# Output filter's channel half mixed on GpSimd and scaled earlier, and the map's six column mixes built on one shared difference

## The chip, the cores and the metric

The kernel runs on one core of one Trainium2 chip. The metric is the device time of one execution in microseconds (us). Before the change three runs took 116.66, 116.89 and 117.22 us; the median is 116.89 us.

## The reference, cut to what matters

Four layers follow each other on a map of 4 images, 128 channels and 16x16 pixels, all in float32. The change lies in the first, which has a spatial attention branch `xs` and a channel attention branch `xc`, and ends with a 3x3 convolution of both:

```python
xs = bn_relu(conv2d(x, w_sam, 1), ...)      # 3x3 convolution
xs = sam(xs, w_qk, w_v, gamma_sam)          # softmax over 256 pixels, per image
xc = bn_relu(conv2d(x, w_cam, 1), ...)      # 3x3 convolution
xc = cam(xc, gamma_cam)                     # softmax over 128 channels, per image
xcat = jnp.concatenate([xs, xc], axis=1)
return conv2d(xcat, w_out, 1)               # 3x3, 256 -> 128 channels
```

`w_out` has two halves: `out_s` works on the spatial branch and `out_c` on the channel branch. The later layers (masked bottleneck, latent attention, a full attention over 256 pixels) are untouched.

## The kernel before, in words

All channels lie on the 128 partitions, so every map of one image is 128x256. The 3x3 convolutions are computed in a transformed form along the width, with three matmuls (one per filter row) for each transformed column set. The output convolution uses sets of four columns: six mixes of the six map columns around each group of four, six mixes of the three filter columns, and an inverse on the results. So before `out_conv` can run, three things have to be made:

- the six mixes of each half of each map, `mixed["s"]` and `mixed["c"]`, by VectorE (DVE) in `mix_columns_six` (L590 to L617). It is called as `s_mixed(0)`, `s_mixed(1)`, `c_mixed(0)`, `c_mixed(1)`, each for two images. Every call has 12 instructions: six read the wide map with a step of four columns (L602 to L605, L612, L613) and write contiguous scratch tiles, and six combine these (L607 to L611, L615, L617).
- four mixes of the filter columns, `w_mix[n]` 0 to 3. Mixes 0 and 1 need the raw columns alone (`mix_weights`). Mixes 2 and 3 need two raw columns scaled by ScalarE (ACT) in `scale_weights` (L427 to L431), and then three more sums (`mix_weights_two`). For `cam` and `out_s` GpSimd (POOL) does this (L329 to L346); for `out_c` DVE does (L619 to L639, called at L765 and L770).
- the other two filter mixes are the raw columns.

Nothing is scheduled by a tool. Each engine has its own program, written out by hand, and runs it in that order; waits are on counters (`wait_ge`). What matters around the change:

- PE (TensorE) interleaves the convolution of `cam` with the spatial attention, and then the output convolution of the spatial half with the channel attention. `s_transpose(b)` (L1132) turns the probabilities of image b once DVE has normalised them; `s_apply(b)` (L1139) waits for ACT's copy of the turned ones; `c_gram(i)` (L1161), `c_transpose(i)` (L1170) and `c_apply(i)` (L1178) are the channel attention of half i.
- DVE runs `s_norm(b)` (L688: one reciprocal, two scalings of 128x256), then `join_outer` of `cam` half 0 (L653), `s_mixed(0)`, `s_residual(2)` and `(3)` (L696), `s_mixed(1)`, `c_max(0)` (L708), `join_inner` of `cam` half 1, `c_norm(0)`, and so on through L739 to L772.
- ACT runs `s_exp(3)`, `s_turned(2)`, `relu_in("cam", 0, ...)` (which waits for L653), `s_turned(3)`, then the channel attention's steps, in which `scale_weights("out_c")` stands after `c_turned(0)` (L459).
- POOL mixes the weights of `cam` and `out_s`, writes one part of `keys` (L348) and is then free until L352, at 79.22 us of the span.

Of the kernel before, what the change touches and what calls it, by code (L numbers as in the profile page):

```python
# [79 lines left out]
def build(nc, x, w_sam, w_cam, w_out, early, late, out):  # L80
    with ExitStack() as ctx:
# [238 lines left out]
        def _(pool):  # L320
# [18 lines left out]
            n, done = "out_s", ev["out_s_w"]  # L339
            pool.wait_ge(ev["out_s_scaled"], 2)  # L340
            pool.wait_ge(done, 3)
            nc.gpsimd.tensor_tensor(w_sum[n][:, :], w_mix[n][:, 2, :], w_mix[n][:, 3, :], ALU.add).then_inc(done, 1)
            pool.wait_ge(done, 4)
            nc.gpsimd.tensor_tensor(w_mix[n][:, 2, :], w_sum[n][:, :], w_raw[n][:, 1, :], ALU.add).then_inc(done, 1)
            nc.gpsimd.tensor_tensor(w_mix[n][:, 3, :], w_sum[n][:, :], w_raw[n][:, 1, :],
                                    ALU.subtract).then_inc(done, 1)  # L346
# [225 lines left out]
        def _(dve):  # L572
# [17 lines left out]
            def mix_columns_six(n, i):  # L590

                d = wide_map[n][:, 2 * i:2 * i + 2, :, :].rearrange("p b h w -> p (b h) w")
                at = [d[:, :, k:k + 4 * (WQ - 1) + 1:4] for k in range(6)]
# [10 lines left out]
                nc.vector.tensor_tensor(four(c), at[4], at[2], ALU.subtract).then_inc(diff, 1)  # L604
                nc.vector.tensor_tensor(four(e), at[3], at[1], ALU.subtract).then_inc(diff, 1)  # L605
                dve.wait_ge(diff, 6 * i + 2)
# [2 lines left out]
                dve.wait_ge(diff, 6 * i + 4)
# [4 lines left out]
                dve.wait_ge(diff, 6 * i + 5)  # L614
                nc.vector.scalar_tensor_tensor(to(0), images(f), 4.0, images(c), ALU.mult, ALU.add).then_inc(done, 1)  # L615
                dve.wait_ge(diff, 6 * i + 6)
                nc.vector.scalar_tensor_tensor(to(5), images(e), 4.0, images(h), ALU.mult, ALU.add).then_inc(done, 1)  # L617

            def mix_weights(n):  # L619
# [8 lines left out]
                                        ALU.subtract).then_inc(done, 1)  # L628

            def mix_weights_two(n):  # L630

                done = ev[f"{n}_w"]
                dve.wait_ge(ev[f"{n}_scaled"], 2)
                dve.wait_ge(done, 3)
                nc.vector.tensor_tensor(w_sum[n][:, :], w_mix[n][:, 2, :], w_mix[n][:, 3, :], ALU.add).then_inc(done, 1)
                dve.wait_ge(done, 4)
# [924 lines left out]
```

## Time and profile before

| | |
|---|---|
| median of three runs | 116.89 us |
| the profiled execution | 117.24 us |
| its span, first to last instruction | 115.4 us |
| PE busy | 107.2 us, 93% |
| DVE busy | 79.1 us, 68% |
| ACT busy | 50.6 us, 44% |
| POOL busy | 16.8 us, 15% |

The span is what the rows below count from. The profiled execution took 1.84 us more than its span, and 0.35 us more than the median. A group of instructions is read as busy time, number and mean duration; a line of the timeline as start, duration, engine, line of the kernel, and in brackets how long the engine sat idle before and what released it. Instructions of one engine overlap slightly, so the distance between starts is less than a duration.

### The profile page before, as it was taken

What the parts mean: (1) busy time and instruction counts of PE and PEld (TensorE: products, weight loads), DVE (VectorE), ACT (ScalarE), POOL (GpSimd) and SP (SyncE); (2) the same over time, 40 slices, a digit from 0 to 9 for tenths busy, and PEclk for the clock granted to TensorE, in tenths of its full rate; (3) what the DMA queues carried; (4) which work ended last, traced back from release to release, by engine and by line L of the source; (5) the groups of instructions that cost most, each with busy time, mean ns of one, the idle gap of its engine ahead of it and who ended that gap; (6) DMA issues with size and microseconds to landing.
All of it is one profiled execution on the core that took longest, in us unless ns stands there. A gap on an engine that the chain in (4) does not pass through costs nothing.

```text
span 115.4 us, 2010 instructions
## 1 busy us (share of the span) xinstructions
PE 107.2 (93%) x699; PEld 91.3 (79%) x699; DVE 79.1 (68%) x249; ACT 50.6 (44%) x147; POOL 16.8 (15%) x28
## 2 busy tenths in 40 slices
PE   5999998989999999989997889998999999999980
PEld 5988887858868989989986579696799997776570
DVE  1756568479899897876967332659564796779960
ACT  5150495997242344130121401014785618769730
POOL 5007995000000000000000000004300002233000
PEclk9999999999999999999999999999999999999999
DMA  3999900000000000000000000000000000000122
GB/s 90 291 354 410 408 31 6 0 0 0 3 0 0 0 3 6 0 0 0 6 0 0 0 0 0 9 0 0 0 0 0 0 6 0 0 0 0 45 70 72
DMA packets 3321, 5.22 MB, mean 45 GB/s; under 512 B 496, under 2 KB 2928, under 8 KB 3184
## 3 DMA queue, kind: packets, MB, share of 16 engines
q1 hardware_dynamic: 3168, 5.09, 12.6%
q8 instruction: 6, 0.10, 0.4%
q10 hardware_dynamic: 144, 0.01, 0.1%
q14 instruction: 3, 0.02, 0.1%
HBM read 4.57 MB, written 0.52 MB: 44 GB/s over the span
## 4 chain that ended last, share of the span: by engine, by line
PE 76%; DVE 11%; ACT 8%; issue 2%; DVEq 0%; ACTq 0%
PE psum L1019 15%; PE psum L1037 9%; PE psum L1103 7%; PE psum L1288 4%; PE psum L1356 4%; PE psum L1330 4%; PE psum L1348 3%; PE psum L1144 2%; PE psum L1401 2%; PE psum L1414 2%; PE psum L1323 2%; PE psum L1242 2%; PE psum L1434 2%; PE psum L1181 2%; PE psum L1338 2%
## 5 line engine op out<-in xcount | busy, mean ns | idle before, releaser
L352 POOL TENSOR_TENSOR att_s<-xc,x 128x256 f32<-128x256 f32 x3 | 2.2, 727 | 61.0 <-DVE xc L891 61.0
L1103 PE MATMUL psum<-spin 128*128 128x256 f32 x50 | 8.9, 336 | 1.2 <-DVE spin L577 1.2
L1103 PEld LDWEIGHTS psum<-spin 128*128 128x128 f32 x50 | 7.8, 233 | 1.5 <-DVE spin L577 1.2
L1019 PE MATMUL psum<-mixed_x,w_raw_sam 128*128 128x256 f32 x24 | 6.8, 436 | 0.0
L358 POOL TENSOR_SCALAR att_c<-x,gbv 128x256 f32<-128x256 f32 x4 | 3.8, 961 | 19.3 <-DVE x L940 19.3
L1019 PE MATMUL psum<-mixed_x,w_mix_cam 128*128 128x256 f32 x24 | 6.4, 384 | 0.0
L1037 PE MATMUL psum<-mixed_s,w_mix_out_s 128*128 128x128 f32 x48 | 6.2, 275 | 0.0
L1019 PE MATMUL psum<-mixed_x,w_raw_cam 128*128 128x256 f32 x24 | 6.2, 379 | 0.0
L1019 PEld LDWEIGHTS psum<-mixed_x,w_raw_sam 128*128 128x128 f32 x24 | 5.4, 231 | 0.9
L1037 PEld LDWEIGHTS psum<-mixed_s,w_mix_out_s 128*128 128x128 f32 x48 | 5.9, 192 | 0.1
L1037 PE MATMUL psum<-mixed_c,w_mix_out_c 128*128 128x128 f32 x48 | 5.7, 275 | 0.0
L1037 PEld LDWEIGHTS psum<-mixed_c,w_mix_out_c 128*128 128x128 f32 x48 | 5.5, 192 | 0.0
L1019 PE MATMUL psum<-mixed_x,w_mix_sam 128*128 128x256 f32 x24 | 5.3, 379 | 0.0
L1356 PE MATMUL psum<-prob,par 128*128 128x128 f32 x32 | 5.2, 286 | 0.1
L587 DVE TENSOR_TENSOR mixed_x<-wide_x 128x256 f32<-128x256 f32 x8 | 3.7, 521 | 2.3 <-DMA wide_x<-in_x 2.3
L914 DVE SCALAR_TENSOR_TENSOR prob<-psum,rinv,par 128x128 f32<-128x128 f32 x16 | 4.9, 347 | 0.3
L1019 PEld LDWEIGHTS psum<-mixed_x,w_mix_sam 128*128 128x128 f32 x24 | 4.6, 190 | 0.6
L1330 PE MATMUL psum<-keys,xc 128*128 128x272 f32 x16 | 4.6, 408 | 0.5 <-ACT keys L492 0.5
L902 DVE TENSOR_REDUCE nmax<-psum 128x2 f32<-128x512 f32 x4 | 2.8, 692 | 3.0 <-PE psum L1330 3.0
L1288 PE MATMUL psum<-hpad,par 128*128 128x256 f32 x18 | 4.2, 384 | 0.6 <-DVE hpad L830 0.6
L1019 PEld LDWEIGHTS psum<-mixed_x,w_raw_cam 128*128 128x128 f32 x24 | 4.3, 190 | 0.5
L1356 PEld LDWEIGHTS psum<-prob,par 128*128 128x128 f32 x32 | 4.2, 191 | 0.3 <-DVE prob L914 0.3
(245 smaller groups left out, 268.8 us busy)
## 6 DMA issues: line engine op xcount, KB each, us to landing
par<-in_late SPq DMA_DIRECT2D x1, 1406.0 KB, 8.0
wide_x<-in_x SPq DMA_DIRECT2D x2, 288.0 KB, 3.9
w_raw_sam<-in_w_sam SPq DMA_DIRECT2D x3, 192.0 KB, 3.5
w_raw_cam<-in_w_cam SPq DMA_DIRECT2D x3, 192.0 KB, 5.1
w_raw_out_s<-in_w_out SPq DMA_DIRECT2D x3, 192.0 KB, 5.2
w_raw_out_c<-in_w_out SPq DMA_DIRECT2D x3, 192.0 KB, 5.1
out<-y SPq DMA_DIRECT2D x2, 128.0 KB, 2.0
out<-y SPq DMA_DIRECT2D x4, 64.0 KB, 2.3
```

Source lines behind the costliest of these rows:

```text
L358: nc.gpsimd.tensor_scalar(x3b[:, b, :], x3[:, b, :], gbv[:, 0:1], None, ALU.add).then_inc(ev["f_xb"], 1)
L587: nc.vector.tensor_tensor(mixed[n][:, k, 2 * i:2 * i + 2, 1:1 + H, :], at[a], at[b], op).then_inc(done, 1)
L902: nc.vector.tensor_reduce(nmax[:, b, :], psum[:, 2 * b:2 * b + 2, L:L + HW], AX.X, ALU.max, negate=True).then_inc(ev["n_max"], 1)
L914: nc.vector.scalar_tensor_tensor(wide[:, b, i, 0:P].rearrange("p (m l) -> p m l", m=M8), o[:, L1 * i:L1 * i + L].unsqueeze(1).broadcast_to ...
L1019: return mm(o[:, c:c + HW].rearrange("p (b s) -> p b s", b=2), w[:, C * dy:C * (dy + 1)], mixed[src][:, i, 2 * half:2 * half + 2, dy:dy + ...
L1037: return mm(o[:, c:c + HALF].rearrange("p (b s) -> p b s", b=2), w[:, C * dy:C * (dy + 1)], mixed[src][:, i, 2 * half:2 * half + 2, dy:dy ...
L1103: mm(bank[k][:, 0:HW], spin[:, 0:P], spin[:, :], start=True, stop=True, skip_group_check=True)
L1144: m = mm(bank[4 + b % 2][:, 0:HW], vt[:, b, j, :], pt_sb[:, b, j, :], start=(j == 0), stop=(j == NCH - 1))
L1288: m = mm(o, par1[:, a + P * t:a + P * (t + 1)], hpad[:, dy:dy + H, dx:dx + W], start=(t == 0), stop=(t == NT - 1))
L1330: m = mm(bank[2 * b + i][:, 0:L + HW], pixels(x2, b, i), keys[:, b, :], start=True, stop=True)
L1348: m = mm(bank[2 * b][:, L1 * i:L1 * (i + 1)], pt_sb[:, b, j, P * i:P * (i + 1)], gt[:, b, j, :], start=(j == 0), stop=(j == NCH - 1))
L1356: m = mm(o[:, 0:HW].rearrange("p (m i c) -> p i m c", i=NCH, c=L)[:, i, :, :], p1("w_o_rep"), wide[:, b, i, 0:P].rearrange("p (m c) -> p m ...
```

## The change

Three edits:

1. GpSimd mixes the weights of `out_c` too. `mix_weights` and `mix_weights_two` become functions on POOL and are called for `out_c` right after `out_s`, before the copy to `keys`. Both are gone from DVE for `out_c` (six instructions of 128x384).
2. ACT's `scale_weights("out_c")` moves from after `c_turned(0)` to after `s_exp(3)`, before `s_turned(2)`.
3. `mix_columns_six` subtracts the map from itself two columns on, once over all 16 columns of every row (128x512), into `mix_t`; the mixes 3, 4, 0 and 5 take every fourth column of that. This replaces four differences of 128x128. The sixth mix comes out with the opposite sign, which the inverse takes back (-1.0 becomes 1.0 in `join_six`).

```diff
@@ gpsimd @@
+            mix_weights("cam")
+            mix_weights("out_s")
+            mix_weights_two("out_s")
+            mix_weights("out_c")
+            mix_weights_two("out_c")
             pool.wait_ge(d_late, 16)
@@ scalar @@
             s_exp(3)
+            scale_weights("out_c")
             s_turned(2)
...
             c_turned(0)
-            scale_weights("out_c")
@@ vector, mix_columns_six @@
+                t = mix_t[n]
+                tk = [t[:, k:2 * H * W:4].rearrange("p (b s) -> p b s", b=2) for k in range(4)]
...
-                nc.vector.tensor_tensor(four(c), at[4], at[2], ALU.subtract).then_inc(diff, 1)
-                nc.vector.tensor_tensor(four(e), at[3], at[1], ALU.subtract).then_inc(diff, 1)
+                nc.vector.tensor_tensor(t[:, :].rearrange("p (r w) -> p r w", w=W), d[:, :, 2:2 + W], d[:, :, 0:W],
+                                        ALU.subtract).then_inc(diff, 1)
...
-                nc.vector.scalar_tensor_tensor(to(3), images(e), 2.0, images(c), ALU.mult, ALU.add).then_inc(done, 1)
-                nc.vector.scalar_tensor_tensor(to(4), images(e), -2.0, images(c), ALU.mult, ALU.add).then_inc(done, 1)
-                nc.vector.tensor_tensor(four(f), at[0], at[2], ALU.subtract).then_inc(diff, 1)
-                nc.vector.tensor_tensor(four(h), at[3], at[5], ALU.subtract).then_inc(diff, 1)
...
-                nc.vector.scalar_tensor_tensor(to(0), images(f), 4.0, images(c), ALU.mult, ALU.add).then_inc(done, 1)
...
-                nc.vector.scalar_tensor_tensor(to(5), images(e), 4.0, images(h), ALU.mult, ALU.add).then_inc(done, 1)
+                nc.vector.scalar_tensor_tensor(to(3), tk[1], 2.0, tk[2], ALU.mult, ALU.add).then_inc(done, 1)
+                nc.vector.scalar_tensor_tensor(to(4), tk[1], -2.0, tk[2], ALU.mult, ALU.add).then_inc(done, 1)
+                nc.vector.scalar_tensor_tensor(to(0), tk[0], -4.0, tk[2], ALU.mult, ALU.add).then_inc(done, 1)
+                nc.vector.scalar_tensor_tensor(to(5), tk[1], -4.0, tk[3], ALU.mult, ALU.add).then_inc(done, 1)
@@ vector, the steps @@
-            mix_weights("out_c")
             c_residual(0)
...
-            mix_weights_two("out_c")
             c_residual(1)
```

The order on POOL, from the last sums of `out_s` on. Before (`w_sum`, `w_mix` and `w_raw` are the sums, the mixed and the raw filter columns; the names behind "waits" are the counters):

```order
L337 TENSOR_TENSOR w_mix_out_s<-w_sum_out_s,w_raw_out_s 128x384
L342 TENSOR_TENSOR w_sum_out_s<-w_mix_out_s 128x384 [waits out_s_w,out_s_scaled]
L344 TENSOR_TENSOR w_mix_out_s<-w_sum_out_s,w_raw_out_s 128x384 [waits out_s_w]
L345 TENSOR_TENSOR w_mix_out_s<-w_sum_out_s,w_raw_out_s 128x384
L348 COPY keys<-par 128x4x16 [waits d_late]
```

and now (the line numbers are those of the changed kernel):

```order
L349 TENSOR_TENSOR w_mix_out_s<-w_sum_out_s,w_raw_out_s 128x384
L334 TENSOR_TENSOR w_sum_out_c<-w_raw_out_c 128x384 [waits d_w_out_c2,d_w_out_c0]
L337 TENSOR_TENSOR w_mix_out_c<-w_sum_out_c,w_raw_out_c 128x384 [waits out_c_w,d_w_out_c1]
L338 TENSOR_TENSOR w_mix_out_c<-w_sum_out_c,w_raw_out_c 128x384
L346 TENSOR_TENSOR w_sum_out_c<-w_mix_out_c 128x384 [waits out_c_w,out_c_scaled]
L348 TENSOR_TENSOR w_mix_out_c<-w_sum_out_c,w_raw_out_c 128x384 [waits out_c_w]
L349 TENSOR_TENSOR w_mix_out_c<-w_sum_out_c,w_raw_out_c 128x384
L358 COPY keys<-par 128x4x16 [waits d_late]
```

Six sums of 128x384 have come between the sums of `out_s` and the copy to `keys`; the fourth of them waits for ACT's scaling.

The order on ACT, from the exponentials of the last image of the spatial attention on. Before:

```order
L401 ACTIVATE prob,rsum<-psum,nmax 128x256 [waits s_max]
L401 ACTIVATE prob,rsum<-psum,nmax 128x256
L407 COPY pt_sb<-psum 128x512 [waits s_tp]
L384 ACTIVATE xc<-eo,bn_shift,bn_inv 128x2x256 [waits cam_y,bn_step]
L407 COPY pt_sb<-psum 128x512 [waits s_tp]
L411 COPY att_c<-psum 128x512 [waits c_yt]
L378 COPY m_sb<-psum 128x256 [waits cam_inner]
```

and now:

```order
L411 ACTIVATE prob,rsum<-psum,nmax 128x256 [waits s_max]
L411 ACTIVATE prob,rsum<-psum,nmax 128x256
L441 ACTIVATE w_mix_out_c<-w_raw_out_c 128x384 [waits d_w_out_c0]
L441 ACTIVATE w_mix_out_c<-w_raw_out_c 128x384 [waits d_w_out_c2]
L417 COPY pt_sb<-psum 128x512 [waits s_tp]
L394 ACTIVATE xc<-eo,bn_shift,bn_inv 128x2x256 [waits cam_y,bn_step]
L417 COPY pt_sb<-psum 128x512 [waits s_tp]
L421 COPY att_c<-psum 128x512 [waits c_yt]
```

The two scalings now stand ahead of the copy of image 2's turned probabilities, and with it ahead of the ReLU of `cam` half 0.

The order on DVE in the first `mix_columns_six`. Before:

```order
L602 SCALAR_TENSOR_TENSOR mix_ab_s<-wide_s 128x128 [waits s_att]
L603 SCALAR_TENSOR_TENSOR mix_ab_s<-wide_s 128x128
L604 TENSOR_TENSOR mix_fech_s<-wide_s 128x128
L605 TENSOR_TENSOR mix_fech_s<-wide_s 128x128
L607 TENSOR_TENSOR mixed_s<-mix_ab_s 128x2x64 [waits s_diff]
L608 TENSOR_TENSOR mixed_s<-mix_ab_s 128x2x64
L610 SCALAR_TENSOR_TENSOR mixed_s<-mix_fech_s 128x2x64 [waits s_diff]
L611 SCALAR_TENSOR_TENSOR mixed_s<-mix_fech_s 128x2x64
L612 TENSOR_TENSOR mix_fech_s<-wide_s 128x128
L613 TENSOR_TENSOR mix_fech_s<-wide_s 128x128
L615 SCALAR_TENSOR_TENSOR mixed_s<-mix_fech_s 128x2x64 [waits s_diff]
L617 SCALAR_TENSOR_TENSOR mixed_s<-mix_fech_s 128x2x64 [waits s_diff]
```

and now:

```order
L614 SCALAR_TENSOR_TENSOR mix_ab_s<-wide_s 128x128 [waits s_att]
L615 SCALAR_TENSOR_TENSOR mix_ab_s<-wide_s 128x128
L616 TENSOR_TENSOR mix_t_s<-wide_s 128x512
L619 TENSOR_TENSOR mixed_s<-mix_ab_s 128x2x64 [waits s_diff]
L620 TENSOR_TENSOR mixed_s<-mix_ab_s 128x2x64
L622 SCALAR_TENSOR_TENSOR mixed_s<-mix_t_s 128x2x64 [waits s_diff]
L623 SCALAR_TENSOR_TENSOR mixed_s<-mix_t_s 128x2x64
L624 SCALAR_TENSOR_TENSOR mixed_s<-mix_t_s 128x2x64
L625 SCALAR_TENSOR_TENSOR mixed_s<-mix_t_s 128x2x64
```

Three instructions fewer; the last four now read `mix_t` with a step of four.

## Rows read from the trace of the kernel before

**Rows 1.** Chain that ended last, in order of time: start us, us, what.

```profile
48.21 0.34 DVE cmax L711
```

**Rows 2.** Timeline, 40 to 75 us: DVE, ACT and PE in the channel attention.

```profile
42.96 0.93 ACT L431 ACTIVATE w_mix_out_c<-w_raw_out_c 128x384 f32<-128x384 f32 x2
...
44.29 0.75 DVE L728 SCALAR_TENSOR_TENSOR wide_c<-psum,par,xc 128x512 f32<-128x512 f32 x1 [0.82 <-PE psum L1181]
...
46.75 1.06 PE L1166 MATMUL psum<-att_c 128*128 128x128 f32 x8
...
48.12 0.43 DVE L711 TENSOR_REDUCE cmax<-psum 128x2 f32<-128x256 f32 x1
...
50.23 0.55 DVE L635 TENSOR_TENSOR w_sum_out_c<-w_mix_out_c 128x384 f32<-128x384 f32 x1
...
50.36 0.44 PE L1175 MATMUL psum<-par,cprob 128*128 128x128 f32 x2 [0.32 <-DVE cprob L723]
...
53.05 0.75 DVE L728 SCALAR_TENSOR_TENSOR wide_c<-psum,par,xc 128x512 f32<-128x512 f32 x1 [1.21 <-PE psum L1181]
```

**Rows 3.** Groups of DVE by line and shape, 36 to 75 us.

```profile
L723 DVE TENSOR_SCALAR cprob<-cprob,cinv 128x128 f32<-128x128 f32 x4 | 1.0, 282 | 0.1
...
L602 DVE SCALAR_TENSOR_TENSOR mix_ab_c<-wide_c 128x128 f32<-128x128 f32 x2 | 0.8, 396 | 0.1
...
L610 DVE SCALAR_TENSOR_TENSOR mixed_c<-mix_fech_c 128x128 f32<-128x128 f32 x2 | 0.6, 290 | 0.0
...
L627 DVE TENSOR_TENSOR w_mix_out_c<-w_sum_out_c,w_raw_out_c 128x384 f32<-128x384 f32 x1 | 0.6, 553 | 0.0
```

**Rows 4.** Timeline, 22 to 41 us: ACT, DVE and PE in the spatial attention.

```profile
22.45 0.41 DVE L677 SCALAR_TENSOR_TENSOR qst<-psum,qst 32x256 fp32r<-32x256 f32 x1 [0.86 <-ACT qst L390]
...
28.67 0.22 ACT L401 ACTIVATION_READ_ACCUMULATOR prob<-psum,nmax 128x1 f32 x1
...
30.01 0.62 DVE L693 TENSOR_SCALAR prob<-prob,rinv 128x256 f32<-128x256 f32 x2
...
30.45 0.59 ACT L407 COPY pt_sb<-psum 128x512 f32<-128x512 f32 x1 [1.55 <-PE psum L1096]
...
30.68 0.60 PE L1096 MATMUL psum<-par,prob 128*128 128x128 f32 x4
30.88 0.75 DVE L653 SCALAR_TENSOR_TENSOR eo<-pq,psum 128x256 f32<-128x256 f32 x2 [0.26 <-PE psum L1019]
...
31.55 0.39 DVE L602 SCALAR_TENSOR_TENSOR mix_ab_s<-wide_s 128x128 f32<-128x128 f32 x1
...
33.09 1.13 PE L1144 MATMUL psum<-pt_sb,vt 128*128 128x256 f32 x4
...
34.60 0.86 DVE L699 SCALAR_TENSOR_TENSOR wide_s<-psum,par,xs 128x256 f32<-128x256 f32 x2
...
39.02 0.42 DVE L711 TENSOR_REDUCE cmax<-psum 128x2 f32<-128x256 f32 x1 [0.39 <-PE psum L1166]
```

**Rows 5.** Timeline, 3 to 22 us: the last sum of out_s on POOL.

```profile
17.73 0.99 POOL L345 TENSOR_TENSOR w_mix_out_s<-w_sum_out_s,w_raw_out_s 128x384 f32<-128x384 f32 x1
```

**Rows 6.** Timeline of DVE, 76 to 83 us: L891 without and with POOL at work.

```profile
78.72 0.42 DVE L891 SCALAR_TENSOR_TENSOR xc<-gate,xs 128x256 f32<-128x256 f32 x1
...
79.51 0.72 DVE L891 SCALAR_TENSOR_TENSOR xc<-gate,xs 128x256 f32<-128x256 f32 x1
```

**Rows 7.** Timeline of POOL, 78 to 83 us.

```profile
79.22 0.73 POOL L352 TENSOR_TENSOR att_s<-xc,x 128x256 f32<-128x256 f32 x1 [60.32 <-DVE xc L891]
```

**Rows 8.** Source L587, the column mixes of x on DVE: duration ns min/median/max.

```profile
L587 DVE TENSOR_TENSOR mixed_x<-wide_x x8: 418/420/1225, 3.7 to 9.4; 128x256 f32<-128x256 f32 x8
```

**Rows 9.** Source L693, the scalings of the spatial attention: ns min/median/max.

```profile
L693 DVE TENSOR_SCALAR prob<-prob,rinv x8: 346/351/354, 21.0 to 30.3; 128x256 f32<-128x256 f32 x8
```

**Rows 10.** Source L965, the same operation in the last layer: ns min/median/max.

```profile
L965 DVE TENSOR_SCALAR prob<-prob,rinv x4: 346/354/485, 101.0 to 106.2; 128x256 f32<-128x256 f32 x4
```

**Rows 11.** Timeline of POOL, 75 us to the end.

```profile
100.99 1.07 POOL L358 TENSOR_SCALAR att_c<-x,gbv 128x256 f32<-128x256 f32 x1 [2.03 <-DVE x L940]
```

More of the change, by code:

```diff
@@ L116, in build @@
         mixed.update({n: sb(f"mixed_{n}", [P, 6, B, HP, WQ]) for n in ("s", "c")})
-        mix_fech = {n: sb(f"mix_fech_{n}", [P, 4, HALF]) for n in ("s", "c")}
+        mix_t = {n: sb(f"mix_t_{n}", [P, 2 * H * W]) for n in ("s", "c")}
         mix_ab = {n: sb(f"mix_ab_{n}", [P, 2, HALF]) for n in ("s", "c")}
@@ L327, in _, with mix_weights @@
             nc.gpsimd.memset(hpad[:, :, :], 0.0).then_inc(ev["zeroed"], 1)
-            for n in ("cam", "out_s"):
+            def mix_weights(n):
                 done = ev[f"{n}_w"]
@@ L338, in _, with mix_weights_two @@
                                         ALU.subtract).then_inc(done, 1)
[L339 to L346, printed above, removed]
+            def mix_weights_two(n):
+                done = ev[f"{n}_w"]
+                pool.wait_ge(ev[f"{n}_scaled"], 2)
+                pool.wait_ge(done, 3)
+                nc.gpsimd.tensor_tensor(w_sum[n][:, :], w_mix[n][:, 2, :], w_mix[n][:, 3, :], ALU.add).then_inc(done, 1)
+                pool.wait_ge(done, 4)
+                nc.gpsimd.tensor_tensor(w_mix[n][:, 2, :], w_sum[n][:, :], w_raw[n][:, 1, :], ALU.add).then_inc(done, 1)
+                nc.gpsimd.tensor_tensor(w_mix[n][:, 3, :], w_sum[n][:, :], w_raw[n][:, 1, :],
+                                        ALU.subtract).then_inc(done, 1)
+            mix_weights("cam")
[3 more added lines that the diff above has]
+            mix_weights_two("out_c")
             pool.wait_ge(d_late, 16)
@@ L593, in mix_columns_six @@
                 at = [d[:, :, k:k + 4 * (WQ - 1) + 1:4] for k in range(6)]
-                f, e, c, h = [mix_fech[n][:, k, :] for k in range(4)]
                 a, b = [mix_ab[n][:, k, :] for k in range(2)]
@@ L603, in mix_columns_six @@
                 nc.vector.scalar_tensor_tensor(four(b), at[1], -4.0, at[3], ALU.mult, ALU.add).then_inc(diff, 1)
[L604 to L606 removed]
+                nc.vector.tensor_tensor(t[:, :].rearrange("p (r w) -> p r w", w=W), d[:, :, 2:2 + W], d[:, :, 0:W],
+                                        ALU.subtract).then_inc(diff, 1)
+                dve.wait_ge(diff, 3 * i + 2)
                 nc.vector.tensor_tensor(to(1), images(a), images(b), ALU.add).then_inc(done, 1)
                 nc.vector.tensor_tensor(to(2), images(a), images(b), ALU.subtract).then_inc(done, 1)
[L609 to L617 removed]
+                dve.wait_ge(diff, 3 * i + 3)
+                nc.vector.scalar_tensor_tensor(to(3), tk[1], 2.0, tk[2], ALU.mult, ALU.add).then_inc(done, 1)
+                nc.vector.scalar_tensor_tensor(to(4), tk[1], -2.0, tk[2], ALU.mult, ALU.add).then_inc(done, 1)
+                nc.vector.scalar_tensor_tensor(to(0), tk[0], -4.0, tk[2], ALU.mult, ALU.add).then_inc(done, 1)
+                nc.vector.scalar_tensor_tensor(to(5), tk[1], -4.0, tk[3], ALU.mult, ALU.add).then_inc(done, 1)
             def mix_weights(n):
@@ L627, in mix_weights @@
                 nc.vector.tensor_tensor(w_mix[n][:, 1, :], w_sum[n][:, :], w_raw[n][:, 1, :],
[L628 to L636, printed above, removed]
-                nc.vector.tensor_tensor(w_mix[n][:, 2, :], w_sum[n][:, :], w_raw[n][:, 1, :], ALU.add).then_inc(done, 1)
-                nc.vector.tensor_tensor(w_mix[n][:, 3, :], w_sum[n][:, :], w_raw[n][:, 1, :],
                                         ALU.subtract).then_inc(done, 1)
@@ L811, in join_six @@
                 dve.wait_ge(ev["out_last"], 2 * i + 2)
-                nc.vector.scalar_tensor_tensor(phase(x1, i, 3), o[:, HALF:HW], -1.0, last[:, i, 1, :], ALU.mult,
+                nc.vector.scalar_tensor_tensor(phase(x1, i, 3), o[:, HALF:HW], 1.0, last[:, i, 1, :], ALU.mult,
                                                ALU.add).then_inc(ev["x1_done"], 1)
```

## Prediction

> **What bounds the kernel now.** I read the chain of waits first: it follows PE nearly everywhere and leaves it only where PE sits waiting. So an edit on another engine is worth what it takes from a wait of PE. I then went through the timeline from 22 to 63 us, where all three edits act, and looked only at PE's idle brackets. Two belong to the change. Before `s_apply(3)`, at 33.09 us, PE waited 0.48 us for ACT's copy of the turned probabilities; that copy stands behind the ReLU, the ReLU behind DVE's L653 at 30.88 us [rows 4]. Before `c_transpose(1)`, at 50.36 us, PE waited 0.32 us for DVE's `c_norm(1)` [rows 2]. The second wait begins in `c_mixed(0)`: the chain passes through `c_max(1)` at 48.2 us [rows 1], and DVE came to it straight from the mixing, without an idle bracket, though `c_gram(1)` had ended at 46.75 + 1.06 = 47.81 us [rows 2].
>
> **The change, part by part.** The sum is made against the profiled execution (117.24 us, span 115.4), which lies 0.35 us above the median of 116.89; I carry the difference over to the median.
>
> *Weights of `out_c` off DVE:* six sums of 0.55 us [rows 3]. Worth nothing: after the first three DVE idled 0.82 us until PE released `c_residual(0)` at 44.29 us, and after the other three (from 50.23 us) it idled 1.21 us until 53.05 us [rows 2]. That cover remains, with more room in it.
>
> *Mixing:* a call takes 34.60 - 31.55 = 3.05 us for 12 instructions [rows 4]. An instruction that reads with a step of four lasts 396 ns, one that reads contiguous scratch 290 ns [rows 3]; from start to start this is about 0.31 and 0.20 us (estimates: each less the overlap of 0.09), and 6 x 0.31 + 6 x 0.20 = 3.06 agrees. Now there are two of the first kind, two of the second, four combinations that read `mix_t` with a step of four, and one subtraction of 128x512. A sum of 128x384 takes 553 ns [rows 3]; 128 elements more at 130 ns (below), less the overlap, give 0.60. The four combinations lie between 0.20 (contiguous) and 0.31 (stepped); I take 0.31, because what rows 3 tell apart is the step of the reads. 2 x 0.31 + 2 x 0.20 + 4 x 0.31 + 0.60 = 2.86 us, 0.19 saved a call; with 0.20 it is 2.42, 0.63 saved. `c_mixed(0)` takes the 0.19 off PE's wait at 50.36 us; more than 48.12 - 47.81 = 0.31 us can't be had there, since `c_gram(1)` is then the later one. `c_mixed(1)` ends long before PE needs it. So this edit is worth **-0.19 us** (bounds -0.31 and 0). The Trainium skill's page "SBUF — State Buffer" (note on cache lines, section "Door 1: The DMA port swizzle") gives "4 fp32" as how far one can step for free. Read so, the combinations would cost 0.20 and the term would be -0.31; the 396 against 290 ns of rows 3 speak against it.
>
> *Scaling on ACT:* two instructions, 0.93 us together [rows 2], in the gap from 28.89 us to the copy at 30.45 us, of which 1.55 us are idle [rows 4]. They end near 29.82 us. Worth nothing where they go and nothing where they leave.
>
> *Weights on POOL:* a sum takes 0.99 us there; the last of `out_s` ends at 18.72 us [rows 5], and the first three of `out_c` follow until 21.8 us. The next three can't start before ACT's scaling has ended. A POOL instruction that waits starts 0.08 us after its releaser (79.22 us against 78.72 + 0.42 [rows 6, 7]): so from 29.9 us, the fifth sum 0.08 us after the fourth, the sixth right behind, undisturbed until 33.0 us, then the copy to `keys` (first read near 80 us). The weights are due at 53.3 us. The duration is covered by 20 us; what counts is what DVE does meanwhile. From 30.01 us it runs the two scalings of `s_norm(3)`, L653, and from 31.55 us `s_mixed(0)` [rows 4].
>
> The trace shows what happens when a POOL sum of two SBUF tensors runs beside a DVE instruction with two SBUF inputs. L891 took 0.42 us alone and 0.72 us when started at 79.51 us beside a POOL sum that ran from 79.22 to 79.95 us [rows 6, 7]: it ended 0.28 us after POOL did, so it did its reading after POOL's end. L587, two SBUF inputs as well, lasted 1225 ns once against 420 [rows 8], beside a POOL sum of the weights. So the instructions of `s_mixed(0)` will be held. For `s_norm(3)` there is no such row: its instruction has one SBUF tensor as input. But it takes 351 ns for 256 elements and 283 for 128 [rows 9, 3], 68 ns per 128, where two-input instructions take 420 - 290 = 130: it moves two elements at a time, so it uses the second path too. Below, its cost is bounded by L965, the same operation, which beside a POOL instruction with one input took 485 ns at most instead of 354, with POOL's at 1072 ns [rows 10, 11]: 0.13 us. Above, by L891: held until POOL's sum has ended. I take the upper one, since POOL's operation is then the same, and it is POOL's that decides how long. The Trainium skill has it as a rule (page "SBUF — State Buffer", section "Who interferes with whom"): an exclusive lock, held for a whole instruction, that a scalar operation of VectorE in its two-port mode takes as well; rows 6 to 8 agree, rows 10 and 11 only in part.
>
> With that: POOL's fourth sum holds from 29.9 to 30.9 us. The first scaling of `s_norm(3)`, due at 30.01, moves its elements until 30.9 + 2 x 0.07 = 31.04 and ends near 31.1. POOL's fifth sum has been ready since 30.98, and goes first; the second scaling ends near 32.3 instead of 30.63 us. L653 then runs from 32.25 to 33.0 (one input in PSUM, not held), the ReLU of 0.86 us from 33.05 to 33.9, ACT's copy to 34.4, and PE starts `s_apply(3)` at 34.4 instead of 33.09: **+1.3 us**. PE's waits from there on have their causes behind this point and shift with it. Is `s_mixed` late too? From 33.05 us, held until 33.3 and once more by the copy to `keys` (0.25), it ends near 36.4; two residuals of 0.9 in all and `s_mixed(1)` of 2.86 lead to 40.2 us, while `c_gram(0)`, which ended near 38.99, has moved to 40.3. Just hidden.
>
> Sum: 1.3 - 0.19 = +1.1 us: 118.3 us for the profiled execution, **118.0 us** for the median.
>
> The first three sums meet only `s_norm(0)` at 20.97 us, which may end 0.7 us late, at 22.3; DVE idled 0.86 us until L677 at 22.45 us [rows 4], and PE turns these probabilities after 23 us. Nothing.
>
> **The rivals.**
>
> *A. POOL keeps the path through its fifth and sixth sum,* which follow each other without a gap. The second scaling then ends near 33.3 us: +2.3 - 0.19, 119.0 us. Against it: L587, of which one instruction was held and not two. 0.08.
>
> *B. DVE gets both scalings in a row after the fourth sum.* `s_norm(3)` ends near 31.4 us, L653 0.55 us late; then `s_mixed(0)` meets the last two sums, ends near 36.2, and `c_max(0)` comes at 39.8 instead of 39.02 us [rows 4]. +0.75 - 0.19, 117.5 us. For it: the two are queued one behind the other, and the decision falls within 0.1 us. 0.13.
>
> *C. `s_norm(3)` is not held* (the 0.13 us of rows 10), only `s_mixed(0)`. Due at 31.55 us, it waits until 32.0, again from 32.3 to 33.3, and 0.2 for the copy: it ends near 36.1 with its own 0.19 saved, against 34.60 us. `c_max(0)` had 0.39 us to spare, and `s_mixed(1)` gives 0.19: 1.3 to 1.5 - 0.39 - 0.19, some +0.8, less 0.19 later, +0.6 at most; if the holds are shorter, +0.4: 117.3 us. 0.23.
>
> *D. Not slower: the collisions fall into DVE's slack.* Between 31.55 us and `c_max(0)` DVE has 0.39 us idle and 2 x 0.19 saved, 0.77 us. If POOL and DVE take turns at some 0.13 us an instruction, as in rows 10 and 11, this covers them, and only the gain at 50.36 us remains: 116.7 us. This decides from the point where DVE loses less than 0.77 us in all, and nothing before L653. Against it: rows 6 to 8, three times the full hold. 0.12.
>
> That the change doesn't do what it says is excluded by the order of the instructions. Faster by more than 0.58 us would need two of PE's waits to fall that no edit touches.
>
> **How the numbers follow.** The forecast has 0.42; 0.02 is left for what no row suggests. Half a per cent, 0.58 us, is about what a measurement of this kernel can tell from no change: the bounds are 116.31 and 117.47 us. Slower: the forecast, A, half of B and a small part of C, 0.59. Same: the rest of B and C, nearly all of D, 0.35. Faster 0.06, the part of D where stepped reads are cheap, and the unknown. Range: 116.6 takes in D and 118.7 the forecast with 0.7 us on top; A is left out, with a little at either end.
>
> **What would show it.** In the profile after: the scalings of image 3 lasting over 1 us (the first to near 31.1, the second to near 32.3 us); PE waiting some 1.3 us or more on either side of `s_apply(3)` for ACT; a scaling of image 0 of about 1 us, harmless; the combinations from `mix_t` at 0.39 us; the wait before `c_transpose(1)` at 0.1 to 0.15 us. It would be wrong if the scalings of image 3 stay at 0.35 us (C or D), or if the sums on POOL, and not the DVE instructions, grow longer.

## The result, and the profile after

| | before | after |
|---|---|---|
| median of 20 runs each | 116.83 us | 117.52 us |
| ratio of the two, 95% interval | | 1.0052 [1.0031, 1.0074] |
| the same, measured again with the experiments | 116.72 us | 117.85 us, 1.0082 [1.0041, 1.0123] |
| a profiled execution, its span | 117.24 us, 115.4 us | 117.59 us, 115.7 us |
| DVE busy | 68% | 66% |
| POOL busy | 15% | 20% |

By the ratios the change makes the kernel slower by 0.6 us (0.5%), by 1.0 us in the second measurement. The forecast was +1.1 us. Some runs of nearly every kernel (8 of these 20 after) had a lower granted clock for a few us from 72 us or later and took 1.4 to 3.3 us more, so the ratios leave them out, the rows here are from a second profile of the changed kernel, whose granted clock was 0.999, and an experiment whose profile was such a run has no milestone for the keys below.

The timeline of the changed kernel, 28 to 52 us, on ACT, POOL, DVE, PE and PE's weight loads (PEld). Columns as ahead of the prediction; L690 are the scalings, L650 is `join_outer`, L394 the ReLU of `cam`, L417 the copy of the turned probabilities, L1139 `s_apply`, L1170 and L1176 `c_transpose` and `c_apply`.

```profile
28.29 0.95 ACT L441 ACTIVATE w_mix_out_c<-w_raw_out_c 128x384 f32<-128x384 f32 x2
29.32 1.00 POOL L346 TENSOR_TENSOR w_sum_out_c<-w_mix_out_c 128x384 f32<-128x384 f32 x1 [8.13 <-ACT w_mix_out_c L441]
29.54 0.94 DVE L690 TENSOR_SCALAR prob<-prob,rinv 128x256 f32<-128x256 f32 x1
30.39 1.15 DVE L690 TENSOR_SCALAR prob<-prob,rinv 128x256 f32<-128x256 f32 x1
30.40 0.99 POOL L348 TENSOR_TENSOR w_mix_out_c<-w_sum_out_c,w_raw_out_c 128x384 f32<-128x384 f32 x1
30.59 0.20 PEld L1091 LDWEIGHTS psum<-par,prob 128*128 128x128 f32 x2 [0.62 <-ACT pt_sb L417]
31.35 1.05 POOL L349 TENSOR_TENSOR w_mix_out_c<-w_sum_out_c,w_raw_out_c 128x384 f32<-128x384 f32 x1
31.47 0.74 DVE L650 SCALAR_TENSOR_TENSOR eo<-pq,psum 128x256 f32<-128x256 f32 x2
31.60 0.20 PEld L1091 LDWEIGHTS psum<-par,prob 128*128 128x128 f32 x2 [0.81 <-DVE prob L690]
32.13 0.53 DVE L614 SCALAR_TENSOR_TENSOR mix_ab_s<-wide_s 128x128 f32<-128x128 f32 x1
32.30 0.87 ACT L394 ACTIVATE xc<-eo,bn_shift,bn_inv 128x512 f32<-128x512 f32 x1 [1.74 <-DVE eo L650]
33.05 0.56 ACT L417 COPY pt_sb<-psum 128x512 f32<-128x512 f32 x1
33.66 0.73 PEld L1139 LDWEIGHTS psum<-pt_sb,vt 128*128 128x128 f32 x4 [0.30 <-ACT pt_sb L417]
...
39.59 0.42 DVE L708 TENSOR_REDUCE cmax<-psum 128x2 f32<-128x256 f32 x1 [0.64 <-PE psum L1161]
...
41.69 0.75 DVE L650 SCALAR_TENSOR_TENSOR eo<-pq,psum 128x256 f32<-128x256 f32 x2
...
42.86 0.85 ACT L394 ACTIVATE xc<-eo,bn_shift,bn_inv 128x512 f32<-128x512 f32 x1 [1.80 <-DVE eo L650]
44.00 1.13 PE L1176 MATMUL psum<-xc,cpt 128*128 128x256 f32 x4 [0.40 <-ACT cpt L432]
...
47.17 0.29 DVE L619 TENSOR_TENSOR mixed_c<-mix_ab_c 128x128 f32<-128x128 f32 x1
...
47.58 0.40 DVE L622 SCALAR_TENSOR_TENSOR mixed_c<-mix_t_c 128x128 f32<-128x128 f32 x1
...
48.53 2.40 PE L1032 MATMUL psum<-mixed_s,w_mix_out_s 128*128 128x128 f32 x20
...
51.03 0.20 PEld L1170 LDWEIGHTS psum<-par,cprob 128*128 128x128 f32 x2 [0.30 <-DVE cprob L720]
51.04 0.44 PE L1170 MATMUL psum<-par,cprob 128*128 128x128 f32 x2
```

**The hold** stands in the first ten rows. POOL's fourth sum runs from 29.32 to 30.32 us; the first scaling of image 3, begun at 29.54, ends at 30.48, 0.16 us after it. The fifth sum runs from 30.40 to 31.39; the second scaling ends at 31.54, 0.15 us after that. Before, the pair took 0.62 us [rows 4]; now the two take 2.00 us. PE's weight loads stand idle twice in `s_transpose(3)`, for 0.62 and 0.81 us, and its matmuls for 0.24 and 0.57 us (the first bracket names ACT's copy, but before that row the program also waits for the first scaling, and the kernel before began the same row while ACT's copy of image 2 was still running: 30.48 against 30.45 + 0.59 us), and `s_mixed(0)` is held once more, L614 taking 0.53 us beside the sixth sum. `c_max(0)` (L708) still waits for PE, 0.64 us against 0.39 [rows 4], so DVE's lateness is over by then. **The mixing**: reads of `mix_t` with a step of four take 0.40 us and contiguous ones 0.29 us.

**What the forecast didn't have** stands at 42.86 us: the ReLU of `cam` half 1 starts 0.42 us after L650 ended (41.69 + 0.75 = 42.44). The ReLU of half 0 starts 0.09 us after its own L650 (31.47 + 0.74 = 32.21, and 32.30). The first profile of the changed kernel has the same 0.42 us. The chain of waits calls it "issue", a wait for nothing that the profile shows:

```profile
41.77 0.67 DVE eo L650 x2
42.45 0.02 issue
42.47 0.02 ACTq L393
42.48 0.38 issue
42.86 0.85 ACT xc L394
```

**Where the time goes.** PE's milestones, counted in every trace from the start of `s_transpose(1)` (first column, in us of the span); the last column is the rest of the span behind the first matmul of the latent attention's keys (L1323 before, L1318 after).

| kernel | start | s_apply(3) | c_transpose(0) | c_apply(0) | c_transpose(1) | keys | rest |
|---|---|---|---|---|---|---|---|
| before | 24.37 | 8.72 | 16.89 | 18.75 | 25.99 | 54.49 | 36.5 |
| before, second profile | 24.19 | 8.72 | 16.88 | 18.74 | 25.99 | 54.47 | 36.3 |
| after | 23.91 | 9.76 | 17.92 | 20.09 | 27.13 | 55.62 | 36.2 |

Between start and keys the change costs 1.13 us, in three steps: **+1.04** before `s_apply(3)`, **+0.31** between `c_transpose(0)` and `c_apply(0)` (2.17 us instead of 1.86), and **-0.20** before `c_transpose(1)` (7.04 instead of 7.24). Two profiles of one kernel agree there to 0.02 us, while start and rest vary by 0.2 us and more between profiles of one kernel; so the experiments are read from this table.

### The profile page after: what moved, and what is told of

The parts are those of the page before. It is cut to its first block, busy times and chain, and to the rows that moved or that the text cites. A ratio compares the mean times of both kernels' runs of the same rounds, so it can differ in the third digit from the quotient of the medians.

```text
span 118.7 us, 1998 instructions
## 1 busy us (share of the span) xinstructions
PE 109.8 (93%) x699; PEld 93.5 (79%) x699; DVE 77.3 (65%) x231; ACT 50.3 (42%) x147; POOL 23.0 (19%) x34
## 4 chain that ended last, share of the span: by engine, by line
PE 73%; DVE 13%; ACT 7%; issue 3%; DVEq 0%; ACTq 0%
PE psum L1014 13%; PE psum L1098 9%; PE psum L1032 8%; PE psum L1325 4%; PE psum L1283 4%; PE psum L1351 3%; PE psum L1343 3%; PE psum L1396 2%; PE psum L1409 2%; PE psum L1429 2%; PE psum L1176 2%; PE psum L1139 2%; PE psum L1333 2%; PE psum L1361 2%; PE psum L1318 2%
## 5 line engine op out<-in xcount | busy, mean ns | idle before, releaser
L1098 PE MATMUL psum<-spin 128*128 128x256 f32 x50 | 11.2, 397 | 1.2 <-DVE spin L587 1.2
L1098 PEld LDWEIGHTS psum<-spin 128*128 128x128 f32 x50 | 9.9, 293 | 1.8 <-DVE spin L587 1.2
L725 DVE SCALAR_TENSOR_TENSOR wide_c<-psum,par,xc 128x512 f32<-128x512 f32 x2 | 1.5, 752 | 5.5 <-PE psum L1176 5.5
```

Of the source, the lines that this page charges most:

```text
L1098: mm(bank[k][:, 0:HW], spin[:, 0:P], spin[:, :], start=True, stop=True, skip_group_check=True)
```

## The experiments

### The changed kernel again, and the kernel before again

Both unchanged, for traces and times beside those of the experiments.

> The changed kernel once more, for its time and for a second trace. Hold theory (POOL's fourth and fifth sums hold the two scalings of image 3): +0.4 to +0.9 us against the kernel before, the two scalings again near 2.0 us together and s_apply(3) about 1.05 us late against the work ahead of it. Rival, ACT stalls: in the first trace ACT started the ReLU of cam half 1 0.42 us after its releaser where it was 0.10 before; if that is part of the change, it is there again and worth 0.3 us, if it was chance it is gone.

Measured: 117.85 us, 1.0082 [1.0041, 1.0123], so +0.5 to +1.4 us. Its rows are those above; the hold and the late ReLU are both there again.

> The kernel before once more, for a second trace: the first trace reached s_transpose(1) at 24.37 us of its span, four traces of other kernels at 22.96 to 24.07 us, though nothing of the change acts ahead of it. If this is chance of the loads, this trace lies among those, near 23.7 us, and from s_transpose(1) to the end it takes the same 91.0 us as the first. If the changed kernels really start earlier, it comes out near 24.4 again. Time: the same as before, within 0.3 us.

Measured: 116.68 us, 1.0012 [0.9978, 1.0045]; its milestones are the second row of the table.

### The mixing alone

`mix_columns_six` as in the change, everything else as before.

> Only the mixing of the map by one difference; the weights of out_c stay on DVE and ACT's scaling where it was. Hold theory: -0.2 us (0.19 a call, of which c_mixed(0) gives its own to PE). Rival, the mixing is what costs (stepped reads slower than the differences they replace): +0.3 us or more.

Measured: 116.39 us, 0.9964 [0.9929, 0.9999]. Milestones: start 22.96; 8.73, 16.89, 18.75, 25.78. The scalings of image 3 are back at 0.62 us and the ReLU of half 1 starts 0.09 us after its releaser. The whole effect in the trace is -0.21 us before `c_transpose(1)`, the forecast's -0.19; the ratio, 0 to -0.8 us, agrees but can't tell the size. The timeline of the kernel with the mixing alone, 45 to 49 us:

```profile
45.30 0.38 DVE L612 SCALAR_TENSOR_TENSOR mixed_c<-mix_t_c 128x128 f32<-128x128 f32 x1
45.60 0.38 DVE L613 SCALAR_TENSOR_TENSOR mixed_c<-mix_t_c 128x128 f32<-128x128 f32 x1
...
46.24 2.40 PE L1035 MATMUL psum<-mixed_s,w_mix_out_s 128*128 128x128 f32 x20
48.74 0.44 PE L1173 MATMUL psum<-par,cprob 128*128 128x128 f32 x2
```

From start to start a combination takes 0.30 us. PE's row of `c_transpose(1)` prints no idle bracket any more, but the row before it ends at 48.64 us (46.24 + 2.40), so 0.10 us of the 0.32 [rows 2] is left.

### The weights alone

The mixing as before; the weights of `out_c` on POOL and the scaling on ACT as in the change.

> Only the weights of out_c on POOL with ACT's scaling after s_exp(3); the map is mixed by the old twelve instructions. Hold theory: slower by 0.2 us more than the full change, so +0.6 to +1.1 us. Rival, the mixing is what costs: 0 to +0.2 us.

Measured: 118.19 us, 1.0139 [1.0088, 1.0190]: +1.6 us, more than the +0.6 to +1.1 expected. Milestones: start 23.63; 9.65, 17.81, 19.98, 27.24, keys 56.10. Both costs are here (the late ReLU too: 2.17 us between `c_transpose(0)` and `c_apply(0)`), without the mixing's gain. Two more stand in its timeline. In the attention of image 0 POOL's third sum starts 0.69 us after DVE's first scaling (20.80 and 20.11 us), where in the changed kernel it starts 0.32 us ahead of it (20.20 and 20.52 us). So two sums hold the two scalings (1.89 us for the pair, where the changed kernel takes 1.09):

```profile
19.84 1.00 POOL L337 TENSOR_TENSOR w_mix_out_c<-w_sum_out_c,w_raw_out_c 128x384 f32<-128x384 f32 x1
20.11 1.89 DVE L692 TENSOR_SCALAR prob<-prob,rinv 128x256 f32<-128x256 f32 x2
20.80 1.04 POOL L338 TENSOR_TENSOR w_mix_out_c<-w_sum_out_c,w_raw_out_c 128x384 f32<-128x384 f32 x1
...
77.20 0.23 DVE L873 SCALAR_TENSOR_TENSOR gate<-gate,cm3q 128x64 f32<-128x64 f32 x1 [1.09 <-ACT gate L491]
77.88 0.43 DVE L881 TENSOR_TENSOR xs<-psum,gate 128x256 f32<-128x256 f32 x1 [0.46 <-DVE gate L873]
...
79.73 0.70 PE L1320 MATMUL psum<-xc,w_keys 128*128 128x256 f32 x2 [0.34 <-ACT xc L497]
```

`s_transpose(1)` is 0.12 us late by that (PE's bracket is 0.30 us, 0.18 in the changed kernel), so the start from which the milestones count is itself late and they come out too small by as much: the forecast's "harmless" scaling of image 0 (1.09 us in the changed kernel) is so only while POOL's third sum starts early enough. The second is PE's wait of 0.34 us before the keys at 79.73 us, where neither edit works. It comes from DVE: L881 starts 0.45 us after its releaser, DVE's own L873, has ended (77.20 + 0.23 = 77.43, and 77.88), where the changed kernel has 0.08 us there. This looks like the late ReLU, on another engine whose program is shorter by the sums taken off it; no run tested that.

### The scaling on ACT later: nothing for POOL to do until then

```diff
             s_exp(3)
-            scale_weights("out_c")
...
             c_exp(0)
+            scale_weights("out_c")
             relu_in("cam", 1, 1, xc, ev["xc_done"])
```

> The full change, but ACT scales the weights of out_c after the exponentials of c_exp(0), so that POOL's last three sums run from about 41.5 to 44.6 us, where DVE reads PSUM or waits. Hold theory: the scalings of image 3 back at 0.35 us each, and the gain of the mixing left alone: -0.2 us against before, 0.8 us under the full change. Rival, it is POOL's first three sums, or the loss of DVE's own sums, or code that lies elsewhere: as slow as the full change, +0.5 us. Rival, ACT's scaling now delays the ReLU behind it: the wait before c_apply(0) grows by up to 0.9 us.

Measured: 116.66 us, 1.0007 [0.9967, 1.0046]. Milestones: start 23.59; 8.73, 16.90, 19.06, 26.08, keys 54.57. POOL's three sums run from 40.61 to 43.66 us, the scalings of image 3 take 0.62 us, and the +1.04 is gone: it was the hold. The expected gain of 0.2 us isn't in the trace, because the ReLU starts 0.41 us after L650's end again. It now stands right behind the scaling, but the scaling doesn't delay it: ACT had been idle for 0.96 us. That sent me to its place in ACT's program.

### Two small copies on ACT

The ReLU of half 1 has two more ACT instructions ahead of it in the changed kernel than before (the scaling's). Three kernels put two copies of 128x1 on ACT behind `s_exp(3)`, in a gap of 1.55 us [rows 4]: one with the mixing alone, one with the later scaling, one with the whole change.

```diff
             s_exp(3)
+            for k in range(2):
+                nc.scalar.copy(pad_out[:, k:k + 1], p0("gam_sam"))
```

> The mixing alone, and two copies of 128x1 on ACT after s_exp(3), in ACT's idle gap, which do nothing but shift ACT's later instructions by two places, as the moved scaling does. Theory P (the extra 0.31 us before c_apply(0) comes from the place of the ReLU of cam half 1 in ACT's program): the 0.31 us appear here too, and eat the gain of the mixing: +0.1 us against before instead of -0.2. Rival (it comes from POOL or from DVE being less busy): no such gap, -0.2 us as with the mixing alone.

> The version with the scaling after c_exp(0), with the same two copies of 128x1 on ACT, so that the ReLU stands four places later than before, not two. Theory P: the 0.31 us go from the ReLU to another instruction; if that one is not waited for, -0.2 us against before, otherwise as the version without them (0.0). Rival: no change.

> The full change with ACT's two copies of 128x1 after its scaling. Theory P: 0.3 us faster than the full change, the wait before c_apply(0) gone; what is left is the hold less the mixing, 1.04 - 0.21 = +0.8 us from s_transpose(1) to the end. Rival (the first two terms are not additive, the hold also feeds the later wait): as slow as the full change.

| kernel | ratio, 95% | ACT instructions more ahead of the ReLU | ReLU after L650's end | c_transpose(0) to c_apply(0) | keys |
|---|---|---|---|---|---|
| mixing alone | 0.9964 [0.9929, 0.9999] | 0 | 0.09 | 1.86 | |
| with two copies | 1.0041 [1.0006, 1.0077] | 2 | 0.42 | 2.17 | 54.57 |
| later scaling | 1.0007 [0.9967, 1.0046] | 2 | 0.41 | 2.16 | 54.57 |
| with two copies | 0.9978 [0.9932, 1.0024] | 4 | 0.10 | 1.85 | 54.26 |
| whole change | 1.0082 [1.0041, 1.0123] | 2 | 0.42 | 2.17 | 55.62 |
| with two copies | 1.0082 [1.0041, 1.0123] | 4 | 0.09 | 1.86 | 55.46 |

The timeline of ACT and DVE, 40 to 44 us; with the mixing alone and two copies:

```profile
40.84 0.74 DVE L654 SCALAR_TENSOR_TENSOR eo<-pq,psum 128x256 f32<-128x256 f32 x2
...
42.00 0.86 ACT L385 ACTIVATE xc<-eo,bn_shift,bn_inv 128x512 f32<-128x512 f32 x1 [1.79 <-DVE eo L654]
...
43.15 1.13 PE L1182 MATMUL psum<-xc,cpt 128*128 128x256 f32 x4 [0.39 <-ACT cpt L423]
```

and with the whole change and two copies:

```profile
41.52 0.75 DVE L653 SCALAR_TENSOR_TENSOR eo<-pq,psum 128x256 f32<-128x256 f32 x2
...
42.36 0.86 ACT L395 ACTIVATE xc<-eo,bn_shift,bn_inv 128x512 f32<-128x512 f32 x1 [1.47 <-DVE eo L653]
```

Two copies in an idle gap some 13 us earlier put the 0.31 us into a kernel without it, and take it out of two kernels with it. So it depends on the ReLU's place in ACT's program. The other kernels here agree: 0.41 us with two instructions more (the weights alone, POOL only writing), 0.10 us with four (the last three below). What lies beneath was not found. This reading rests on the traces: the ratios move by +0.9, -0.3 and 0.0 us from row to row of a pair, and with intervals of 0.4 to 0.5 us to either side they can't show 0.31 us.

The whole change with copies gained only 0.16 us at the keys, and nothing by its ratio, where 0.3 us were expected: the copies stand before the scaling and make POOL's fourth sum later against DVE (29.16 us, where the pair of scalings starts at 29.19 and takes 2.19 us), so `s_apply(3)` comes at 9.94 instead of 9.76. POOL is later against DVE by 0.19 us and `s_apply(3)` by 0.18: the hold answers to the time of POOL's sums, nearly one to one.

### POOL only writes

```diff
+                if n == "out_c":
+                    for k in range(3):
+                        nc.gpsimd.memset(fill[:, k, :], 0.0).then_inc(done, 1)
+                    return
```

> The full change with POOL's last three sums for out_c left out; in their place, behind the same waits, three fills of 128x1100 with zeros of about 1 us each, which read nothing. The mixes 2 and 3 of out_c are so never finished. Hold theory: what holds DVE is POOL's reading; then the instructions of s_mixed(0), with two inputs, are not held at all. For the scalings of image 3, which move two elements at a time, reads and writes may both count: held as before (2.0 us together) if POOL's writes are enough, 0.62 us together if not. Rival (DVE is slowed by whatever POOL does): both are held.

This kernel leaves out the last three sums of `out_c`, so its mixes 2 and 3 stay unfinished. One run, 120.74 us at a granted clock of 0.971; only its timeline, 28 to 36 us, is read:

```profile
29.84 3.28 POOL L349 MEMSET fill<- 128x1100 f32 x3 [8.46 <-ACT w_mix_out_c L446]
...
30.08 2.09 DVE L695 TENSOR_SCALAR prob<-prob,rinv 128x256 f32<-128x256 f32 x2
...
32.74 0.39 DVE L619 SCALAR_TENSOR_TENSOR mix_ab_s<-wide_s 128x128 f32<-128x128 f32 x1
```

The pair of scalings is held as long by POOL's writes (2.09 us) as by its sums, so it isn't reads alone that hold them. L619, with two inputs in SBUF, takes its usual 0.39 us while the third fill still runs. The Trainium skill's page "SBUF — State Buffer" (section "Who interferes with whom") has both: VectorE's two-port mode, in which a scaling moves two elements at a time, meets anything GpSimd does, two SBUF inputs meet only its reads. These rows agree.

### The scaling of image 3 in a form that isn't held

```diff
+                if b == 3:
+                    for i in range(NCH):
+                        nc.vector.tensor_scalar(prob[:, b, i, :], prob[:, b, i, :], rinv[:, b, i:i + 1], 0.0,
+                                                ALU.mult, ALU.add, accum_out=unused[:, i:i + 1]).then_inc(ev["s_norm"], 1)
+                    return
```

(and the two copies on ACT).

> The full change with ACT's two copies of 128x1 (so without the 0.31 us of the ReLU's place), and the two scalings of image 3 given an accumulator output that nobody reads, so that they should move one element at a time (about 0.42 us each instead of 0.35, and a short read behind each). Hold theory: they are then not held by POOL (both done within 1.1 us, s_apply(3) at most 0.3 us late), and only s_mixed(0) is, beside the fifth and sixth sum: c_transpose(0) 0.4 to 0.7 us late, the whole +0.2 to +0.5 us. Rival (any DVE instruction that reads SBUF is held beside POOL's sums): 2 us together as before, the whole +0.8 us.

Measured: 116.95 us, 1.0012 [0.9979, 1.0045]. Milestones: start 23.42; 8.71, 17.19, 19.05, 26.07. The timeline:

```profile
29.02 1.01 POOL L348 TENSOR_TENSOR w_sum_out_c<-w_mix_out_c 128x384 f32<-128x384 f32 x1 [7.47 <-ACT w_mix_out_c L443]
29.05 0.48 DVE L695 TENSOR_SCALAR_CACHE_REDUCE prob<-prob,rinv 128x256 f32<-128x256 f32 x1
...
29.45 0.48 DVE L695 TENSOR_SCALAR_CACHE_REDUCE prob<-prob,rinv 128x256 f32<-128x256 f32 x1
...
30.59 0.77 DVE L618 SCALAR_TENSOR_TENSOR mix_ab_s<-wide_s 128x128 f32<-128x128 f32 x1
31.29 1.20 DVE L619 SCALAR_TENSOR_TENSOR mix_ab_s<-wide_s 128x128 f32<-128x128 f32 x1
...
40.61 0.44 PE L1179 MATMUL psum<-par,cprob 128*128 128x128 f32 x2 [0.20 <-DVE cprob L729]
```

With the sum written out beside it, a scaling takes 0.48 us instead of 0.35 [rows 9] and runs straight through POOL's fourth sum; `s_apply(3)` is back at 8.71. The Trainium skill's same page and section excepts this form from the two-port mode; the 0.48 us agree. Now `s_mixed(0)` is held instead, 0.77 + 1.20 us for two instructions of 0.39. DVE is late, and `c_transpose(0)` comes 0.30 us later than before, less than the 0.4 to 0.7 expected. This is rival C as a kernel of its own: +0.30 - 0.2, where the forecast gave it +0.4 to +0.6.

### POOL waits for a better moment

The scaling on ACT stays where the change has it, with the two copies. POOL's last three sums wait.

```diff
             mix_weights("out_c")
+            pool.wait_ge(ev["c_exp"], 2)
             mix_weights_two("out_c")
```

> As the one before, with one wait more: POOL starts its last three sums only after the exponentials of c_exp(0), near 40.5 us; ACT's scaling stays after s_exp(3). Hold theory: when POOL runs is all that matters; the scalings of image 3 at 0.62 us together, and -0.2 us against before (1.0 us under the kernel without the wait). Rival (ACT's scaling, or the missing sums on DVE, have a share): between 0 and +0.8 us.

Measured: 117.64 us, 0.9983 [0.9941, 1.0024]. Milestones: start 23.47; 8.74, 17.54, 19.39, 26.42. The hold of image 3 is gone (0.62 us, `s_apply(3)` at 8.74), and between this kernel and the whole change with copies lies one wait. But the expected gain is missing from the trace, which is 0.43 us longer than before at `c_transpose(1)`. The ratio goes by five of the thirteen runs; the eight with a granted clock of 0.995 or more have a median of 116.81 us, the 27 such runs of the kernel before 116.52 us, and that +0.3 us agrees with the trace. The timeline, 39 to 42 us:

```profile
39.68 0.99 POOL L347 TENSOR_TENSOR w_sum_out_c<-w_mix_out_c 128x384 f32<-128x384 f32 x1 [18.28 <-ACT cprob L428]
39.84 0.92 DVE L724 TENSOR_SCALAR cprob<-cprob,cinv 128x128 f32<-128x128 f32 x1
40.68 0.27 DVE L724 TENSOR_SCALAR cprob<-cprob,cinv 128x128 f32<-128x128 f32 x1
40.75 1.06 POOL L349 TENSOR_TENSOR w_mix_out_c<-w_sum_out_c,w_raw_out_c 128x384 f32<-128x384 f32 x1
41.01 0.44 PE L1174 MATMUL psum<-par,cprob 128*128 128x128 f32 x2 [0.74 <-DVE cprob L724]
```

The same event that releases POOL releases DVE's `c_norm(0)`. POOL is 0.16 us quicker and holds the first scaling until 40.76 us. The second is not held, and here POOL's fifth sum is the longer one (1.06 us). In the changed kernel the second scaling starts 0.01 us before the fifth sum and is held; here it starts 0.07 us before it and isn't. The scalings here are also half as long (128 elements, not 256), so these two traces don't show whether 0.06 us of start or the length decides which goes first.

> As the kernel in which POOL waits for c_exp(0), but it waits for c_norm(0), the step behind it. That kernel's trace showed its first late sum starting with the two scalings of c_norm(0) and holding them, with c_transpose(0) 0.65 us late. Hold theory: now POOL's sums run from about 41.3 to 44.3 us, beside instructions of DVE that read PSUM, and nothing is held: c_transpose(0) back at 16.9 us after s_transpose(1), c_transpose(1) at 25.8, and -0.2 us against before, as with the scaling after c_exp(0) and the two copies. Rival (ACT's early scaling or DVE's missing sums have a share): 0.2 us or more over that.

The same with `ev["c_norm"]` in place of `ev["c_exp"]`. Measured: 116.37 us, 0.9972 [0.9942, 1.0001]. Milestones: start 23.08; 8.66, 16.82, 18.69, 25.71.

```profile
39.37 0.48 DVE L724 TENSOR_SCALAR cprob<-cprob,cinv 128x128 f32<-128x128 f32 x2
39.93 1.00 POOL L347 TENSOR_TENSOR w_sum_out_c<-w_mix_out_c 128x384 f32<-128x384 f32 x1 [18.63 <-DVE cprob L724]
```

From image 3 on nothing is held, and the trace is 0.28 us shorter than before at `c_transpose(1)`. Of this 0.06 us is a late start: image 0's scalings took 1.83 us here, and PE's bracket before `s_transpose(1)` is 0.24 us instead of 0.18. The other 0.22 us is the mixing's. So neither ACT's early scaling nor the sums missing on DVE has a share in the +1.04 us, which was the rival. All three edits of the change are in this kernel. By its ratio it is 0.3 us under the kernel before, which the interval just can't tell from no change, and about 1 us under the changed kernel. The kernels with ratios of 0.9978 and 0.9983 can't be told from it by time; in the traces it is ahead of the second by 0.7 us and level with the first.

## Why the prediction was right, and where its sizes were off

- **Outcome.** 117.52 us lies in the range of 116.6 to 118.7 us, and the kernel is slower, as the likeliest case had it; by 0.6 us, only just over the 0.58 us named as the bound, with an interval (+0.4 to +0.9 us) that reaches to both sides of it. The predicted 118.0 us is 0.5 us too long. In the traces the change costs 1.13 us up to the keys, which is the forecast's 1.1 by luck: a hold 0.26 us too large stands against a late ReLU of 0.31 us that the forecast didn't have.
- **The hold of `s_norm(3)`, +1.3 us: right in kind, 0.26 us too large.** On the clock of the old trace (0.46 us later) the fourth sum starts at 29.78 us, not 29.9, because the fill-in on ACT ended earlier; and I had put the end of the second scaling 0.33 us behind that of the fifth sum, where it lies 0.15 us behind. `s_apply(3)` falls on 34.13 instead of 34.4 us. The kernel with the later scaling and the two whose POOL waits show that the whole of it is the hold: 8.73, 8.74 and 8.66 instead of 9.76 and 9.94. One reading of the old trace was off without harm: the 0.48 us before `s_apply(3)` were idle time of PE's weight loads, while its matmuls stood still for 0.09 us there (32.41 + 0.59 = 33.00, and 33.09).
- **The order of fifth sum and second scaling: right, by little.** I had the fifth sum go ahead, since it is ready first. In the changed kernel the two start 0.01 us apart. Rival B (both scalings in a row) didn't come, but the kernel whose POOL waits for `c_exp` shows that order, with shorter scalings.
- **The mixing, -0.19 us: right** (-0.21 alone, -0.20 in the change). Combinations take 0.38 to 0.40 us, 0.30 from start to start, so stepped reads cost what they cost before. The "4 fp32" of the Trainium skill's page "SBUF — State Buffer" (note on cache lines, section "Door 1: The DMA port swizzle") as a step that is free doesn't hold here: 0.40 us against 0.29. PE's wait before `c_transpose(1)` is 0.11 us (48.53 + 2.40 = 50.93, and 51.04), as forecast.
- **Weights off DVE and scaling on ACT, 0 each: the first right, the second wrong.** With the weights on POOL, the later scaling and two copies, `c_transpose(1)` comes at 49.57 - 23.80 = 25.77 us after the start, with the mixing alone at 25.78. ACT's two instructions cost nothing in their gap and nothing where they left, as rows. But they moved the ReLU of half 1 two places in ACT's program, and this costs 0.31 us. This is the step that failed. No row of the old trace has it, since there both ReLUs start 0.10 us after their releasers.
- **`s_mixed` just hidden: right.** L708 waits 0.64 us for PE. No instruction of `s_mixed(0)` was held by more than 0.14 us, and it ended at 35.22 us, 35.68 on the old clock, against the 36.4 us of the forecast. Hidden with room to spare, then.
- **Scaling of image 0: right** in the changed kernel (1.09 us), but not safe: with the weights alone it took 1.89 us and cost 0.12, with POOL waiting for `c_norm` 1.83 us and 0.06.
- **Rivals.** A (path through the sixth sum) fell: the second scaling came through after the fifth. C fell in the change, since the scalings are held; as a kernel of its own it costs 0.08 us at `c_transpose(1)`, less than I gave it. D fell: DVE lost far more than its slack before `s_apply(3)`.
- **What stays open.** The terms in the trace add up to +1.04 + 0.31 - 0.20 = +1.15 us, 1.13 at the keys. The ratios give +0.6 and +1.0 us in two measurements, and from the start of `s_transpose(1)` to the end of the span the traces have 91.0 and 90.8 us before and 91.8 us after. The traces of the changed kernel start `s_transpose(1)` at 23.91 and 24.07 us, those of the kernel before at 24.37 and 24.19 us; but kernels whose program is the same up to there lie at 22.96 and 24.09 us, so two traces don't show that the change starts earlier. I can't say where the difference goes. Nor is it settled why the ReLU starts late at one place in the program and not two places on, nor whether DVE's late L881 with the weights alone has the same cause.

## What to carry to other kernels

Before work goes to an idle GpSimd, ask not whether it has the time but what VectorE does beside it: each sum of 128x384 there holds a scaling or a two-input instruction until about 0.1 to 0.25 us after its own end, and if that instruction stands on TensorE's path, a 20 us reserve on GpSimd is worth nothing. Release such work with a wait on the end of the critical steps (here `c_norm(0)`), not on the event that also releases VectorE. And when an edit moves TensorE by some 0.3 us at a place it doesn't touch, shift the program of the engine that starts late by two small instructions (here ACT's) before explaining the edit.
